# Self-attention scores of one tile made by 32-row, 64-column parts of the array in two rounds; expert rows blanked only behind each expert's last row

## What is computed

```python
att = jnp.einsum('bhqd,bhkd->bhqk', q, k) / jnp.sqrt(jnp.float32(hd))
causal = jnp.tril(jnp.ones((T, T), bool))
att = jnp.where(causal, att, -jnp.inf)
att = jax.nn.softmax(att, axis=-1)
y = jnp.einsum('bhqk,bhkd->bhqd', att, v)
...
top_v, top_i = jax.lax.top_k(logits, TOP_K)
for e in range(NUM_EXPERTS):
    mid = jax.nn.gelu(flat @ exp_W1[e] + exp_b1[e], approximate=False)
    out = out + w_full[:, e:e + 1] * (mid @ exp_W2[e] + exp_b2[e])
```

## Time and profile before

| | us |
|---|---|
| runs | 672.19, 674.15, 679.93 (median 674.15) |
| profiled execution | 669.32 |
| its span | 667.2 |
| eight beats end, table and scatters end, first row load | 484, 500, 501.5 |

### The profile page before, as it was taken

One profiled execution on the slowest core, in us unless ns is written; L12 is line 12 of the kernel. 1 busy time (PEld: TensorE's weight loads), 2 busy tenths in 40 slices (PEclk: granted clock), 3 DMA queues, 4 the chain that ended last, 5 costly groups with the idle time before them and its releaser, 6 DMA issues.

```text
span 667.2 us, 13654 instructions
## 1 busy us (share of the span) xinstructions
PE 519.1 (78%) x4384; PEld 426.9 (64%) x4384; DVE 423.2 (63%) x1340; ACT 232.5 (35%) x558; POOL 321.7 (48%) x343
## 2 busy tenths in 40 slices
PE   0455897987989888789889889888507999999950
PEld 0443585666667566467567567666407999999940
DVE  4544765787587697688788687664443555555436
ACT  0312323314324424233333333233104556655620
POOL 4502532652464582584484474466361555555530
PEclk9976977989888898799699599597557999999985
DMA  4999660270090090072000000001016677767629
GB/s 108 192 161 219 118 82 2 55 106 1 9 153 10 23 161 10 26 134 34 20 4 0 20 13 2 16 17 33 12 52 180 187 225 201 213 209 211 203 86 330
DMA packets 90481, 64.08 MB, mean 96 GB/s; under 512 B 16302, under 2 KB 77105, under 8 KB 90420
## 3 DMA queue, kind: packets, MB, share of 16 engines
q1 hardware_dynamic: 86100, 54.86, 38.2%
q0 software_dynamic: 4320, 8.47, 3.7%
HBM read 35.18 MB, written 28.58 MB: 96 GB/s over the span
## 4 chain that ended last, share of the span: by engine, by line
PE 54%; DVE 18%; POOL 10%; issue 8%; ACT 3%; SPq 3%; DMA 2%; DVEq 1%; POOLq 0%; ACTq 0%
PE bank L674 10%; PE bank L684 9%; PE bank L529 5%; PE bank L504 5%; POOL sorted_rows L978 4%; PE bank L388 4%; PE bank L383 3%; PE bank L516 3%; PE bank L487 2%; POOL km L958 2%; DVE places L1065 2%; PE bank L447 2%; POOL rs L909 2%; PE bank L502 2%; SPq L307 1%
## 5 line engine op out<-in xcount | busy, mean ns | idle before, releaser
L1042 POOL DMA_INDIRECT result_rows<-back,rows x71 | 69.8, 982 | 76.9 <-DVE back L1463 76.0
L844 ACT ACTIVATE mid<-bank,b 128x128 f32<-128x128 f32 x284 | 80.9, 369 | 52.8 <-PE bank L674 52.8
L529 PEld LDWEIGHTS bank<-vbd,pT 128*128 128x128 f32 x512 | 73.6, 213 | 38.7 <-issue 26.5
L958 POOL TENSOR_TENSOR km<-kb,head 128x512 f32<-128x512 f32 x56 | 59.7, 1072 | 63.4 <-ACT kb L752 48.8
L529 PE MATMUL bank<-vbd,pT 128*128 128x36 f32 x512 | 72.9, 292 | 11.5 <-ACT pT L765 9.5
L909 POOL TENSOR_TENSOR rs<-ve,minus_half 128x4 f32<-128x4 f32 (+1 forms) x40 | 45.5, 1144 | 66.1 <-DVE ve L1149 35.3
L674 PE MATMUL bank<-hT,w 128*128 128x128 f32 x568 | 76.9, 280 | 0.3 <-DVE hT L1453 0.3
L765 ACT COPY pT<-bank 128x512 f32<-128x512 f32 x64 | 37.4, 585 | 109.1 <-PE bank L516 109.0
L684 PE MATMUL bank<-w,mid 128*128 x568 | 74.9, 275 | 0.0
L978 POOL DMA_INDIRECT sorted_rows<-send,slot_u x64 | 62.9, 982 | 18.0 <-issue 18.0
L388 PE MATMUL bank<-ident,places 128*128 128x128 f32 x160 | 34.4, 358 | 47.2 <-DVE places L1065 21.8
(11 more groups left out here) (186 smaller groups left out, 935.3 us busy)
## 6 DMA issues: line engine op xcount, KB each, us to landing
w<-in_L_ffn_exp_W_dram SPq DMA_DIRECT2D x79, 256.0 KB, 3.6
sorted_rows<-blank SPq DMA_DIRECT2D x64, 260.0 KB
rows<-sorted_rows SPq DMA_DIRECT2D x71, 65.0 KB
places<-result_rows SPq DMA_DIRECT2D x16, 256.0 KB, 5.4
places<-in_ctx_dram SPq DMA_DIRECT2D x8, 256.0 KB, 3.0
places<-in_x_dram SPq DMA_DIRECT2D x8, 256.0 KB, 3.4
out_dram<-acc SPq DMA_DIRECT2D x8, 256.0 KB, 6.2
result_rows<-back,rows POOLq DMA_INDIRECT x71
```

Source lines behind the costliest of these rows:

```text
L529: last = pe.matmul(pv_bank[:, hp * W:hp * W + W].rearrange("p (b c) -> p b c", b=BPT), pT[:, j, :], vbd[u][:, t, :, hp, :], start=True, st ...
L844: A(mid[s][:, c, :], hidden[2 * s + c // 2][:, c % 2 * P:c % 2 * P + P], ACT.Gelu, bias=b1[:, bass.ds(expert, 1), c]).then_inc(mid_ok, 1)
L958: G.tensor_tensor(km[n % 2][:, :, :], kb[u][:, n % 2, t * S:t * S + S].unsqueeze(1).broadcast_to([P, HG, S]), head8[:, :].unsqueeze(2).bro ...
L1042: G.indirect_dma_start(out=result_dram, out_offset=bass.IndirectOffsetOnAxis(ap=rows[s][:, D:D + 1].bitcast(U32), axis=0), in_=back[s % 4] ...
```

## The change

- A tile's scores are made together, for all 16 heads and both sequences. Queries `qs` and keys `kb` stay as the projection left them, 128 features by 512 tokens, one instruction each on DVE and ACT. `km` is now masked keys of one tile, four heads wide for both sequences: every quarter of 32 rows holds its own four heads. So POOL masks three tiles a beat instead of seven units, and DVE one.
- `part_scores` makes four products of 32 rows, 64 output columns and 256 moving columns: round 0 uses row quarters 0 and 2, round 1 quarters 1 and 3, each for both column halves. Quarters 0 and 1 write one bank, 2 and 3 the other. `first_scores` puts both masks and does round 0; `other_scores` waits for it by a new semaphore `s0_ps` and does round 1.
- The order on PE: first scores and other scores of the next tile stand in odd slots, on either side of the transposes; both subtractions of a tile stand at the head of the even slot. In slot 0 the next group's projections stand behind the first and the other scores. `first_scores` waits for the exponentials of both units. DVE finds both maxima in a row.
- No fill. A region is 128 rows longer. DVE adds count and region start (`tail_of`), SP reads the eight numbers and writes 128 blank rows at each, and waits for them (`blanked`) before the first rows are loaded.

```diff
+    REGION = TOKENS + P
-    SPARE = E * TOKENS
+    SPARE = E * REGION
...
-        kb = lanes("kb", [P, 2, T * S])
-        qbd = lanes("qbd", [P, 2, T, P])
-        km = lanes("km", [P, HG, S])
+        kb = lanes("kb", [P, N])
+        qs = lanes("qs", [P, N])
+        km = lanes("km", [P, BPT, HR, S])
...
+        def masked_keys(eng, u, t):
+
+            return eng.tensor_tensor(
+                km[t % 2][:, :, :, :],
+                kb[u][:, t * P:t * P + P].rearrange("p (b s) -> p b s", b=BPT).unsqueeze(2).broadcast_to([P, BPT, HR, S]),
+                head4[:, :].unsqueeze(1).unsqueeze(3).broadcast_to([P, BPT, HR, S]), ALU.mult)
...
-                def fill(u, group):
-                    for e in range(E):
-                        sp.dma_start(sorted_v[group][:, e, :, :], blank[:, :].unsqueeze(1).broadcast_to([P, T, ROW]))\
-                          .then_inc(filled[u], 16)
...
+                sp.wait_ge(tails_ok, 1)
+                for e in range(E):
+                    tail = sp.value_load(tail_of[0:1, e:e + 1], min_val=e * REGION, max_val=e * REGION + TOKENS)
+                    sp.dma_start(sorted_dram[bass.ds(tail, P), :], blank[:, :]).then_inc(blanked, 16)
                 for u in LANES:
                     sp.wait_ge(scattered[u], GROUPS // 2 * 2 * T * 16)
+                sp.wait_ge(blanked, E * 16)
...
-                    pe.matmul(bank_n[:, :], ident_bf[:, :], causal[:, :].unsqueeze(1).broadcast_to([P, HG, S]),
-                              start=True, stop=False)
-                    pe.matmul(bank_n[:, :], qbd[u][:, n % 2, n // 2, :], km[n % 2][:, :, :],
-                              start=False, stop=True).then_inc(s_ps, 1)
+                def part_scores(k, u, t, i):
+                    part = slice(i * HR * S, (i + 1) * HR * S)
+                    for b in range(BPT):
+                        for g in range(2):
+                            r = slice((2 * g + i) * ROWS, (2 * g + i + 1) * ROWS)
+                            last = pe.matmul(score_bank[g][half(b), part],
+                                             qs[u][r, t * P + b * S:t * P + b * S + S],
+                                             km[t % 2][r, b, :, :], start=False, stop=True,
+                                             skip_group_check=True)
+                    return last
+
+                def first_scores(k, u, t):
+                    if t == 0:
+                        pe.wait_ge(qbd_ok, k + 1)
                         pe.wait_ge(km0_ok, k + 1)
                     else:
+                        pe.wait_ge(km_ok, k * (T - 1) + t)
+                    if not (isinstance(k, int) and k * T + t == 0):
+                        pe.wait_ge(p_ok, k * UNITS + 2 * t)
+                    for g in range(2):
+                        pe.matmul(score_bank[g][:, :], ident_bf[:, :],
+                                  causal[:, :].unsqueeze(1).broadcast_to([P, HG, S]), start=True, stop=True)
+                    part_scores(k, u, t, 0).then_inc(s0_ps, 1)
+
+                def other_scores(k, u, t):
+                    pe.wait_ge(s0_ps, k * T + t + 1)
+                    part_scores(k, u, t, 1).then_inc(s_ps, 1)
...
-                        scores(k, u, 0)
-                    subtract_max(k, n)
-                    if n + 1 < UNITS:
-                        if not (isinstance(k, int) and k * UNITS + n == 0):
-                            pe.wait_ge(p_ok, k * UNITS + n)
-                        scores(k, u, n + 1)
+                        first_scores(k, u, 0)
+                        if nxt:
+                            project_k(nxt[0])
+                        other_scores(k, u, 0)
+                        if nxt:
+                            project_q(nxt[0])
+                    if n % 2 == 0:
+                        subtract_max(k, n)
+                        subtract_max(k, n + 1)
...
+                    if n % 2 and n + 1 < UNITS:
+                        first_scores(k, u, n // 2 + 1)
                     probs_T(k, n)
+                    if n % 2 and n + 1 < UNITS:
+                        other_scores(k, u, n // 2 + 1)
...
+                    A(kb[u][:, :], F1[:, :], ACT.Identity, bias=cols[:, BK]).then_inc(kf_ok, 1)
...
+                    V.tensor_scalar(qs[u][:, :], F2[:, :], cols[:, BQ], SCALE, ALU.add, ALU.mult).then_inc(qbd_ok, 1)
...
+                    if n % 2 and n + 1 < UNITS:
+                        score_max(k, n + 1)
+                        score_max(k, n + 2)
```

More of the change, by code:

```diff
@@ L34, in xattn_attention_moe @@
     HG = HEADS // 2
+    HR = HEADS // 4
+    ROWS = HR * HD
     UNITS = 2 * T
@@ L749, in keys @@
                     act.wait_ge(kf_ps, k + 1)
-                    for g in range(2):
-                        for b in range(BPT):
-                            last = A(kb[u][half(b), g, :].rearrange("p (t s) -> p t s", t=T),
-                                     F1[half(g), :].rearrange("p (t b s) -> p t b s", t=T, b=BPT)[:, :, b, :],
-                                     ACT.Identity, bias=cols[half(g), BK])
-                        last.then_inc((kb0_ok, kf_ok)[g], 1)
+                    A(kb[u][:, :], F1[:, :], ACT.Identity, bias=cols[:, BK]).then_inc(kf_ok, 1)
                 def exp_scores(k, n):
@@ L901, in _ @@
                     keep(causal[half(b), :], MASKED, ALU.is_ge, 0, [[-1, S]], 1)
-                    keep(head8[half(b), :], 0.0, ALU.is_ge, 0, [[-HD, HG]], 1)
-                    keep(head8[half(b), :], 0.0, ALU.is_ge, HD - 1, [[HD, HG]], -1)
                     step(G.memset(batch2[half(b), b:b + 1], 1.0))
+                for r in range(4):
+                    own = slice(r * ROWS, (r + 1) * ROWS)
+                    keep(head4[own, :], 0.0, ALU.is_ge, 0, [[-HD, HR]], 1)
+                    keep(head4[own, :], 0.0, ALU.is_ge, HD - 1, [[HD, HR]], -1)
                 step(G.memset(kvz[:, :, :, :, :], 0.0))
@@ L996, in slot @@
                         scatter_waits(*routed)
-                    for unit_n in {0: (2,), 1: (3,), 3: (6,), 4: (7,)}.get(n, ()):
-                        head_keys(k, u, unit_n)
+                    if n == 3:
+                        head_keys(k, u, 3)
                     if prev and n == 3:
@@ L1179, in unit0_keys @@
                 def unit0_keys(k, u):
-                    dve.wait_ge(kb0_ok, k + 1)
+                    dve.wait_ge(kf_ok, k + 1)
                     if not (isinstance(k, int) and k == 0):
-                        dve.wait_ge(s_ps, k * UNITS - 1)
-                    V.tensor_tensor(km[0][:, :, :], kb[u][:, 0, 0:S].unsqueeze(1).broadcast_to([P, HG, S]),
-                                    head8[:, :].unsqueeze(2).broadcast_to([P, HG, S]), ALU.mult).then_inc(km0_ok, 1)
+                        dve.wait_ge(s_ps, k * T - 1)
+                    masked_keys(V, u, 0).then_inc(km0_ok, 1)
                 def queries(k, u):
                     dve.wait_ge(qf_ps, k + 1)
-                    for g in range(2):
-                        for b in range(BPT):
-                            last = V.tensor_scalar(
-                                qbd[u][half(b), g, :, b * S:b * S + S],
-                                F2[half(g), :].rearrange("p (t b s) -> p t b s", t=T, b=BPT)[:, :, b, :],
-                                cols[half(g), BQ], SCALE, ALU.add, ALU.mult)
-                        last.then_inc(qbd_ok, 1)
+                    V.tensor_scalar(qs[u][:, :], F2[:, :], cols[:, BQ], SCALE, ALU.add, ALU.mult).then_inc(qbd_ok, 1)
                 def self_values(k, u):
@@ L1395, in block_table @@
                                     ALU.mult).then_inc(table, 1)
-                    V.tensor_scalar(jump[:, :], n_blocks[:, :], -float(P), float(TOKENS), ALU.mult, ALU.add).then_inc(table, 1)
+                    V.tensor_scalar(jump[:, :], n_blocks[:, :], -float(P), float(REGION), ALU.mult, ALU.add).then_inc(table, 1)
                     then(4)
```

58 lines of the change are left out of this document (18 added, 40 removed).

## The result

The changed kernel takes 727.81 us (median of four runs, 718.47 to 739.29), the kernel before 673.69 beside it (672.19 to 679.93): ratio 1.070, 95% interval 1.055 to 1.085. Every ratio here is taken over the runs within 1.5% of their kernel's fastest, which leaves out the two slowest runs of the changed kernel (the two medians alone would give 1.080). Slower was forecast, but 697 us was too little, and the time lies just above the range (726). The profiled execution took 718.47 us.

A forecast was written before the change was run, and what follows sets the result against it. PE was taken to bound eight attention beats (one group of four tiles, about 52 us each). Order +2.0 and clock +1.0 a beat: 8 x 3.0 - 1.3 = +23, so 697 us as a median; range 670 to 726.

The forecast's parts named there:

- the clock: PE in attention beats: lumped waits bring more half-clock time, costing 1.0 us a beat, bounds 0 and 2.5.
- Tile scores 2.0 us: PE, attention scores: masks, small products four abreast and two mode rounds take 2.0 us a tile, against 2.16 before.
- rival B: PE's small score tiles don't run four abreast: 724 us with two abreast, 779 one by one; chance 0.15.
- Key waits, -1.7: PE's two waits a beat for masked keys from POOL go, 1.67 us less.
- Maxima waits in three of four tiles: PE's subtraction waits near 1 us for DVE's maxima in three of a beat's four tiles.
- Copy waits: PE's probability products wait for ACT's copy of the transposes just before them, 0.8 us at each of two places.
- Wait at the queries 1.5 to 3 us: PE waits 1.5 to 3 us, instead of 0.62, for the next group's normalised queries before their transposes.
- Order and tiles +2.0 us a beat: Attention beat: no gain up to the query transposes, then more scores (+0.8) and new waits (+1.2), +2.0 us.
- Fill, 0: Deleting the blank fill gains the beats nothing, since beats with and without it both took 52.0 us.
- First beat, -1.3: First attention beat: writing the queries in fewer DVE instructions gains 1.3 us once.
- A: Rival: PE's waits go, nothing replaces them, the chain to the queries moves forward; 654 us, chance 0.11.
- C: Rival, no change: order costs 2.0 a beat, clock nothing, tiles 1.75 us, chain 0.5 earlier; 677 us, chance 0.11.

The follow-up runs named there:

- the full products with the clock held: Kernel before with its full score products but the changed kernel's order, no fill, 27 wide spare products a beat: 704.34 us, ratio 1.032.
- the fed old order: Kernel before without the fill, with 12 spare products of 512 columns in the waits at each beat's end: 668.61 us, ratio 0.983.
- with the clock held: Changed kernel with 27 wide spare products a beat, 17 in mid-beat and 10 at its end: 676.45 us, ratio 1.003.
- the doubled round: Changed kernel with every small score product issued twice, so that masked scores come out doubled: 785.98 us, ratio 1.157.
- the thin-fed kernel: Changed kernel with 26 spare products of 36 columns a beat in PE's mid-beat waits: 761.97 us, ratio 1.123.

## Why the prediction came out as it did

**The step that failed is the clock.** I took 1.0 us a beat for it, bounds 0 and 2.5. In PE's busy time the lower clock costs about 7 us a beat, by another base 9; in the beat's length about 4 are left, since a slower PE waits less. The working from the six beats: the kernel's own work at the full clock is 38.8 us a beat in the new kernel and, by the full products with the clock held (49.4 busy less 10.0 spare), 39.4 in the old; measured busy times are 51.6 and 45.3. Half clock stretched the first by 12.8 and the second by 5.9 us, 6.9 more. With 0.6 less work and 0.2 less idle time that gives the 6.1 by which a beat grew. (By the fed old order the old work is 41.4 us, 44.7 busy less 3.3 spare, at a clock of 0.97; then the stretch grew by 8.9 and the work shrank by 2.6.) In the terms of the forecast, the beat grew by 6.1 us, and with the clock held the order and tiles cost at most 1.9 (below): that leaves at least 4.2 for the clock where I had 1.0. I had priced the clock as one more low stretch of 3.5 us behind a lump of waits. It is a stretch of some 20 us, which goes on long after the waits, under work that keeps PE nearly always busy. My source, showed a fall after waits, and I took the length of the stretch from it too, and from the shorter of its two rows: the other is 10.5 us, worth up to 5.2 us a beat. Even two short stretches, 3.5 us by my own sum, lie beyond the bound of 2.5.

What I missed is what held the clock before: the full score product, two records of 512 columns over all 128 rows, eight times a beat. The change takes all of them away. I priced that as time saved and never as what held the clock. In the same order, full products have the clock at 0.85 with 9.1 us of idle time a beat, small ones at 0.75 with 6.9. But the products are not the whole loss: the new order with full products already takes 4.2 of the 6.1 us, half as waits and half as clock. Which part of the thin work lets the clock fall (transposes, 36-column products, small tiles) was not parted.

**Point by point.**
- *Tile scores 2.0 us*: 1.71. Four abreast was right (rival B is out: 0.59 us a round, 3.8 abreast when doubled). Of the 0.6 us that I had put down for getting in and out of the two rounds, some 0.3 are there (2 x 0.59 less 0.85). The Trainium skill, TensorEngine Tiling (Array Packing), section Tiling Modes, has a change of mode drain the engine; the trace agrees that it costs something, 0.14 to 0.16 us a round (with the 56 ns a record of the doubled round, or with the 0.85 us a tile).
- *Key waits, -1.7*: gone, as forecast.
- *Maxima waits in three of four tiles*: one in a beat, 0.9. Elsewhere other work, or the half clock itself, may have given DVE the time; no run parts the two.
- *Copy waits*: three, 2.0 us in all; 1.6 was put down.
- *Wait at the queries 1.5 to 3 us*: 1.1.
- *Order and tiles +2.0 us a beat*: with the clock held and spare work in both, 53.0 us against 51.1 of the fed old order, +1.9. But the ratio 1.003 over 0.983 holds 7 more us of mid-beat spare work a beat, of which an unknown part fell into waits, so this is an upper bound rather than a proof. Its parts are larger and opposite: about +4.6 for the order and that feed (55.7 against 51.1), -2.7 for the small tiles.
- *Fill, 0*: 0.85%, 5 to 6 us in favour of the change.
- *Tails, 0*: right; the eight took 8.25 us of SP for the 9 estimated, beside the scatters.
- *First beat, -1.3*: it took 60.7 us against 58.0, so 2.7 the other way.

**The rivals.** A and C (faster, no change) needed the clock to stay as it was. With it held, the changed kernel is at 1.003, the number of C, but that does not bear C out: its clock is then 0.98, where C assumed the 0.89 of before. Against the old order with its end fed, at 0.97, it is 1.003 over 0.983, 2% slower: nearer to my order term of 2.0 us a beat than to C's 0.5.

The Trainium skill, TensorE: Matmul & The Clock Gate, Part 1, says that the clock is set by how busy PE has been of late. With busy read as the profile's busy share, the trace does not agree: it shows a stretch at 0.52 with PE busy 19.18 of 21.0 us, and 26 thin spare products in the gaps changed nothing.

## What to carry to other kernels

Before you shrink or pack a dense product, ask whether it is what holds TensorE's clock: price the rest of the stage at half clock as a case of its own, and look at the granted clock beside the busy share, for a busy PE at 0.52 is not a fast one. If the clock is the suspect, put wide spare products into the waits: two runs, one wide and one thin, tell density from idleness, and the gain of the wide one is the least that the clock costs. And an order that needs two banks at once gives up the unit of work that stood between a reduction and its use; here that cost more than the packed products gave (some 4 us a beat against 2.7).

## What the runs showed of the hardware that was not expected

- TensorE ran 20 us at half clock while busy 91% of the time, mostly with transposes, 36-column products and small tiles; in the thin-fed kernel the beats were 94% busy at 0.75.
- Doubling the 32 by 64 tile products left the clock at 0.73; 17 products of 184 columns on the whole array, about 7 us of a 55 us beat, lifted it from 0.75 to 0.92 (58 to 480 us), and ten of 512 columns more to 0.98 from the second beat to the eighth.
- Small-tile records of 256 columns cost 56 ns each, 3.8 abreast, once the round has begun; a round of eight takes 0.59 us, so beginning and ending it costs about 0.14 us by this rate.
- With the same order on PE, full 512-column score products kept the clock at 0.85 with 9.1 us of idle time a beat, small ones at 0.75 with 6.9.
- In the waits at the old kernel's beat end, 12 products of 512 columns raised the clock from 0.86 to 0.93 (58 to 480 us); whether 24 of 32 columns raised it (0.88) is within what executions of one kernel differ by.
